# The gates' variance kept in a PSUM bank, and one Newton step written with the variance as a factor of its first operation

## What is computed

```python
x = x + conv(_ln_c(x), Wk, bk, Wq, bq, Wv, bv, Wr, br)      # linear attention, 8 heads, over the 16384 pixels
t = _to_tokens(x)                                           # (4, 16384, 64)
t = t + ffn(_ln_t(t), router_w, router_b, expert_w, expert_b)

def _ln_t(v, eps=1e-05):
    return (v - v.mean(-1)) / sqrt(v.var(-1) + eps)

def ffn(x, ...):                                            # B, N, D, C, E, K = 8, 4096, 64, 64, 8, 2
    router_probs = softmax(x @ router_w + router_b)
    top_p, top_i = top_k(router_probs, K); top_p /= sum(top_p)
    return sum over the two chosen experts of top_p * (x @ expert_w[e] + expert_b[e])
```

## Time and profile before

| | |
|---|---|
| median of 3 runs | 662.58 us (661.94 to 663.03) |
| profiled execution, its own time | 661.13 us |
| its span (first to last instruction) | 659.3 us |
| PE busy | 612.2 us (93%) |
| DVE busy | 506.5 us (77%) |
| ACT busy | 420.3 us (64%) |
| POOL busy | 396.4 us (60%) |
| granted TensorE clock, mean over the span | 0.991 |

### The profile page before, as it was taken

How to read it: one execution, slowest core, us unless ns; L and a number is a source line. 1 busy time by engine, 2 the same in 40 slices (tenths; PEclk the granted TensorE clock), 3 DMA queues, 4 the chain that set the end, 5 groups by cost and what they waited for, 6 DMA issues and landing times.

```text
span 659.3 us, 21452 instructions
## 1 busy us (share of the span) xinstructions
PE 612.2 (93%) x8318; PEld 277.4 (42%) x8318; DVE 506.5 (77%) x1176; ACT 420.3 (64%) x800; POOL 396.4 (60%) x350
## 2 busy tenths in 40 slices
PE   3799989779999999999999999999999999999997
PEld 1566656444444444444444444444333333332232
DVE  3434444798888888898888888988798999989954
ACT  2265646576767676766676676775857667676552
POOL 7223252127666566667666566656677767777986
PEclk9999989799999999999999999999999999999999
DMA  6132535395555566655556665544565667545652
GB/s 151 33 100 67 146 100 130 81 226 132 139 131 138 141 158 160 145 134 127 145 129 147 146 162 129 129 120 109 133 150 135 145 159 176 130 96 120 151 132 49
DMA packets 32663, 86.22 MB, mean 131 GB/s; under 512 B 7650, under 2 KB 7826, under 8 KB 32562
## 3 DMA queue, kind: packets, MB, share of 16 engines
q1 hardware_dynamic: 32082, 84.64, 53.4%
q0 software_dynamic: 288, 0.19, 0.2%
q10 hardware_dynamic: 192, 0.01, 0.0%
HBM read 34.47 MB, written 16.78 MB: 78 GB/s over the span
## 4 chain that ended last, share of the span: by engine, by line
PE 72%; DVE 18%; issue 6%; ACT 2%; POOL 2%; DVEq 0%; ACTq 0%; POOLq 0%
PE bank L1103 28%; PE bank L1089 8%; PE bank L1026 6%; PE bank L1004 5%; PE bank L990 5%; DVE z L834 4%; PE bank L949 3%; PE bank L973 3%; PE bank L1050 3%; PE bank L1100 3%; DVE x L734 2%; DVE osb L844 2%; PE bank L1075 2%; DVE xnT L689 2%; DVE bank L749 1%
## 5 line engine op out<-in xcount | busy, mean ns | idle before, releaser
L442 POOL TENSOR_TENSOR z<-gbs,x1d 128x512 f32<-128x512 f32 x256 | 320.6, 1278 | 170.8 <-ACT gbs L579 78.0
L1106 PE MATMUL bank<-z,ew 128*64 128x512 f32 x512 | 244.6, 599 | 0.0
L1103 PE MATMUL bank<-z,ew 128*64 128x512 f32 x512 | 243.6, 598 | 0.0
L579 ACT COPY gbs<-bank 128x512 f32<-128x512 f32 x256 | 140.9, 595 | 46.4 <-PE bank L1089 46.0
L834 DVE TENSOR_TENSOR z<-bank,x1d 128x512 f32<-128x512 f32 x256 | 165.3, 678 | 6.3 <-PE bank L1089 6.3
L433 POOL TENSOR_TENSOR xsq<-xin 128x512 f32<-128x512 f32 x64 | 65.4, 1044 | 85.0 <-DMA xin<-in_x_dram 67.4
L1103 PEld LDWEIGHTS bank<-z,ew 128*64 128x64 f32 x512 | 64.9, 136 | 103.4 <-issue 96.9
L1089 PE MATMUL bank<-grows,sel 64*64 64x512 f16 x1024 | 85.7, 387 | 6.1 <-ACT grows L573 4.8
L503 ACT COPY xn<-bank 128x512 f32<-128x512 f32 x64 | 34.4, 590 | 62.4 <-PE bank L949 62.4
L1106 PEld LDWEIGHTS bank<-z,ew 128*64 128x64 f32 x512 | 64.4, 136 | 1.1 <-POOL z L442 1.1
L734 DVE SCALAR_TENSOR_TENSOR x<-bank,br_col,x_again 128x512 f32<-128x512 f32 x64 | 45.0, 745 | 20.0 <-PE bank L1050 20.0
(11 more groups left out here) (135 smaller groups left out, 819.9 us busy)
## 6 DMA issues: line engine op xcount, KB each, us to landing
x1d<-x SPq DMA_DIRECT2D x128, 256.0 KB, 4.5
xin<-in_x_dram SPq DMA_DIRECT2D x64, 256.0 KB, 4.2
x_again<-in_x_dram SPq DMA_DIRECT2D x64, 256.0 KB, 4.1
out_dram<-osb SPq DMA_DIRECT2D x128, 128.0 KB, 2.6
k<-in_const_dram SPq DMA_DIRECT2D x1, 453.5 KB, 4.0
ew_nat<-in_L_ffn_expert_w_dram POOLq DMA_DIRECT2D x2, 64.0 KB, 6.4
sel<-in_const_sel_dram SPq DMA_DIRECT2D x1, 128.0 KB, 3.3
bk_rows<-bk_wide ACTq DMA_DIRECT2D x6, 1.0 KB, 1.7
```

Source lines behind the costliest of these rows:

```text
L442: pool.tensor_tensor(z[:, 1, i % R_Z, :], gbs[:, i % R_Z, :], x1d[:, g % 2, 1, u * NT:(u + 1) * NT], ALU.mult).then_inc(z_pool, 1)
L579: nc.scalar.copy(gbs[:, i % R_Z, :], bank[:, :]).then_inc(taken_of(("spread", i, 1)), 1)
L1103: pe.matmul(out_bank[0:C, :], ew[:, j, :], z[:, 0, i % R_Z, :], start=False, stop=(j == PAIRS - 1), skip_group_check=True).then_inc(prod_d ...
L1106: pe.matmul(out_bank[C:P, :], ew[:, j, :], z[:, 1, i % R_Z, :], start=False, stop=(j == PAIRS - 1), skip_group_check=True).then_inc(prod_d ...
```

## The change

The variance goes to a third strip of `dev_work` in bank 7 and no longer to `bstat[:, 1]` in SBUF. The three operations of Newton's step compute the same product in another order: before, -0.5 * r * r, times the variance, then plus 1.5 and times r; now -0.5 * variance * r, times r, then plus 1.5 and times r. The number of instructions, their order on every engine, their shapes and their semaphores stay as they are. Three of the 27 gate steps have operands in another memory:

| step | before | now |
|---|---|---|
| 2, clamp and epsilon | bank to SBUF | bank to bank |
| 3, reciprocal | SBUF to SBUF | bank to SBUF |
| 4, first of Newton | SBUF, SBUF to bank | bank, SBUF to bank |
| 5, second of Newton | bank, SBUF to bank | the same |

The other use of `newton`, for the statistics of x, is not touched, nor is step 0 (L749), whose two inputs are both in SBUF.

```diff
-        dev_work = [bank[7][:, QG * E + QG * i:QG * E + QG * (i + 1)] for i in range(2)]
+        dev_work = [bank[7][:, QG * E + QG * i:QG * E + QG * (i + 1)] for i in range(3)]
...
-                def rooted():
-                    dve.wait_ge(dev_root, p + 1)
-                    return dev[0]()
-
...
+                def gate_root():
+                    dve.wait_ge(dev_root, p + 1)
+                    return dve.scalar_tensor_tensor(dev_work[0], dev_work[2], -0.5, bstat[:, 3, :], ALU.mult, ALU.mult)
+
...
-                dev = newton(bstat[:, 0, :], bstat[:, 3, :], bstat[:, 1, :], dev_work)
                 steps = [
                     start,
                     lambda: dve.tensor_tensor(halves(dev_work[1]), halves(dev_work[0]), square, ALU.add),
-                    lambda: dve.tensor_scalar(bstat[:, 1, :], dev_work[1], 0.0, EPS_FFN, ALU.max, ALU.add),
-                    lambda: dve.reciprocal(bstat[:, 2, :], bstat[:, 1, :]),
-                    rooted, dev[1], dev[2],
+                    lambda: dve.tensor_scalar(dev_work[2], dev_work[1], 0.0, EPS_FFN, ALU.max, ALU.add),
+                    lambda: dve.reciprocal(bstat[:, 2, :], dev_work[2]),
+                    gate_root,
+                    lambda: dve.tensor_tensor(dev_work[1], dev_work[0], bstat[:, 3, :], ALU.mult),
+                    lambda: dve.scalar_tensor_tensor(bstat[:, 0, :], dev_work[1], 1.5, bstat[:, 3, :],
+                                                     ALU.add, ALU.mult),
```

## The result

| | before | changed | ratio (95% interval) |
|---|---|---|---|
| first comparison | 662.26 us (4 runs, 660.60 to 663.03) | 654.30 us (4 runs, 653.77 to 655.33) | 0.9885 (0.9862 to 0.9908) |
| second | 660.86 (17 runs) | 655.18 (6 runs) | 0.9908 (0.9883 to 0.9933) |
| third | 661.51 (11 runs) | 654.69 (6 runs) | 0.9894 (0.9865 to 0.9924) |
| fourth | 661.81 (17 runs) | 653.94 (5 runs) | 0.9885 (0.9848 to 0.9922) |

The fourth row is without one run of 662.26 us in the slow state. The kernel is faster, by 8.0, 5.7, 6.8 and 7.9 us.

What follows compares the result with a forecast made beforehand. PE was taken to set the pace, with VectorE mattering only where PE stops for it. Five quads at 1.22 us, 6.1 us in all, off the median 662.58 gave 656.5 us, range 655.3 to 660.3.

Steps and rivals of the forecast that it cites:

- The two holds: In five quads, gate step 4 and L657 on x's statistics wait for POOL's products; 0.97 and 1.03 us would go.
- the second rival: The hold doesn't depend on where inputs are, so new step 4 waits as before: 662.6 us, chance 0.03.
- `scale` gives part of it back: L767, two SBUF inputs, now comes inside POOL's second product and waits: 0.29 of step 4's 0.97 us given back.
- The second hold: L657 on x's statistics now passes before POOL's next pair in five quads, 1.03 us sooner; margin 0.57 us.
- the first rival: L657 on x's statistics still meets POOL's next pair, so nothing is gained: 662.6 us, chance 0.09.
- the form: The rival that the hold doesn't depend on where step 4's inputs lie: nothing gained, 662.6 us, chance 0.03.
- some of the five: Only some of the five held quads lose their stops; with half left 3.1 us gained, 659.5 us, chance 0.09.
- What PE makes of it: PE gains only its waits at L1036, L1089 and L966: 1.22 us in each of five quads, 6.1 us.
- The sum's base: The gain of 6.1 us was taken from the median of the runs, 662.58 us, giving 656.5.
- Steps 2 and 3: Gate clamp bank to bank, no change within 10 ns; reciprocal from the bank 4 ns longer; zero in the sum.
- The slower rival: The hold moves to untouched step 0 (L749) in the seven middle quads: +2.8 to +4.8 us, about 666, chance 0.05.

Runs made afterwards that it cites:

- order_only: The changed kernel with the variance back in SBUF and the new order of Newton's step kept: 661.46 us, ratio 1.0006 to the kernel before.
- four copies: The changed kernel with four unused bank-to-SBUF copies (128 x 160) on DVE ahead of the bias in five quads: 669.78 us, ratio 1.0109 to the kernel before.

## Why the prediction was right in its mechanism and missed its range

*The two holds.* Right. Step 4 no longer waits in any quad, and the row of the variance in SBUF brings the old time back. That the hold depends on two SBUF inputs rested on the association of rows before. It is shown now by step 4 in both forms (`order_only` differs from the changed kernel in the place of the variance alone), and step 0 in both forms agrees, though there the operation changed with its input. One reading of the prediction was wrong: the last Newton operation of the gates (L657, 191 to 192 ns) was not in POOL's company. POOL was busy during one of its 16 executions, and at 215.34 it stood idle between 215.02 and 216.67. So that row was next to no evidence, and the second rival deserved more than its 0.03; step 4 of the changed kernel is what tells, since POOL was busy beside eight of its 16 executions and none lasts over 200 ns. What stands ahead of the prediction, that the engines meet only at semaphores, is too narrow by this hold, which no semaphore shows (and not all engines write to SBUF here, as it has it: every PE row writes a bank). The page "SBUF — State Buffer" of the Trainium skill, in the section on SBUF's two separate sides, states it as a lock: a VectorE instruction with two SBUF inputs and a GpSimd instruction that reads SBUF exclude each other for a whole instruction, whichever starts first. The traces here agree for POOL in front (its products read `gbs` and `x1d` in SBUF); no run here singles out the other case. There is one addition: between two held operations in a row POOL gets in a whole product (1.18 and 1.19 us).

*`scale` gives part of it back.* Right: 0.70 us in the five quads, from 214.61 + 0.81 = 215.42 on.

*The second hold goes because DVE passes L657 ahead of POOL's pair, margin 0.57 us.* Right, and this was the step on which the gain hung. 0.48 us of added work left it alone and 0.72 brought it back with the whole time. So the first rival, that nothing is gained, comes true as soon as the margin is used up, and the 0.09 that it got was no formality. The rivals "the form" and "some of the five" didn't occur.

*What PE makes of it.* Here a term of the sum was mis-sized, 5 x 1.22 = 6.1 us where 6.65 was measured. I took 1.22 us a quad from the idle times in brackets. The start of L749 in two neighbouring quads gives what a quad takes. Before, with 212.22 from the earlier trace rows:

```profile
249.63 0.38 DVE L749 SCALAR_TENSOR_TENSOR bank<-lg 128x32 f32<-128x32 f32 x1
```

Changed:

```profile
213.03 0.38 DVE L749 SCALAR_TENSOR_TENSOR bank<-lg 128x32 f32<-128x32 f32 x1
```

```profile
249.12 0.39 DVE L749 SCALAR_TENSOR_TENSOR bank<-lg 128x32 f32<-128x32 f32 x1
```

37.41 against 36.09 us: 1.32 a quad, and 6.65 over the five, not 6.1. A PE wait is counted from the end of the last matmul, and an unheld matmul starts before that end: L1038 starts 0.64 us behind a group that lasts 0.71. The bracket of 0.83 us was a loss of 1.54 - 0.64 = 0.90. Over the whole stretch, from the transposition to the first expert product behind the three stops, before and changed:

```profile
222.40 0.59 PE L1103 MATMUL bank<-z,ew 128*64 128x512 f32 x1
```

```profile
221.65 0.59 PE L1105 MATMUL bank<-z,ew 128*64 128x512 f32 x1
```

222.40 - 217.89 = 4.51 against 221.65 - 218.70 = 2.95 us: the three stops of 1.22 us by their brackets cost 1.56. About 0.24 of it goes again some 6 us later, mostly where PE now starts the queries (L992, was L990) 0.36 and then 0.48 us behind the matmul before and not 0.24 and 0.43; what it waits for there was not followed up.

*The sum's base.* This is the larger part of the miss. I moved everything to the median of three runs, 662.58, which was a high one: with the fourth run it is 662.26, and in the three later comparisons the kernel before has 660.86, 661.51 and 661.81. From their mean of 661.4, less 6.65, comes 654.7, and the 21 runs of the changed kernel behind the four medians have one of 654.6. So of the 1.9 us between forecast and median about 1.2 are the base and about 0.5 the size of the term. The range had 0.5 us on the low side for the term, which was just enough, and 0.55 for the scatter, which was not.

On the profiled execution I forecast 655.0 us, and it took 655.33. That this fits is luck. With a gain of 6.65 it should have been 654.5, but the two profiles differ in the start as well. Between step 0 at 140 us and the next one, ahead of the seven quads, the kernel before took 35.2 us and the changed one 36.6. The granted clock between 140 and 150 us was full in the one and 0.83 in the other:

```profile
140.00:150.00 10.00, 8.53 (x177) 5.11 (x179) 8.05 (x23) 8.60 (x17) 3.85 (x4) 1.00 0.93 223
```

```profile
140.00:150.00 10.00, 8.52 (x145) 4.80 (x146) 7.63 (x20) 8.02 (x16) 3.43 (x3) 0.83 0.92 220
```

0.17 of 10 us would fit the 1.4 us, but the clock isn't the whole story. In the second comparison's profile of the changed kernel the clock was full there, and the stretch still took 36.5 us; PE stood for 1.27 us at L1006, for nothing that the profile shows:

```profile
150.79 0.97 PE L1006 MATMUL bank<-xnT,keys 128*64 128x66 f32 x25 [1.27 <-issue]
```

Of the twelve profiles of all kernels ten took 36.4 to 36.7 us for this stretch, and only those of the kernel before and of the changed one in the fourth comparison 35.2. So the profile on which the sum was built was a favourable one by 1.4 us. That is why the changed kernel's profile shows 5.8 us of gain with 6.65 in the five quads. What sets this stretch to one or the other stays open.

*Steps 2 and 3.* Right: the reciprocal from the bank takes 357 ns, and step 2 takes 199 ns where it took 191. The estimated 65 ns by the page "VectorE: DVE Perf Modes" of the Trainium skill, section on the TRN2 errata, don't show; the reciprocal is 4 ns longer.

*The slower rival.* L749 was held no longer than before (0.38 at 213.03), so DVE and POOL did move with PE. But slower was nearer than I thought, by another way: four copies, 0.97 us of DVE work where the margin is 0.57, give two holds in a row and 1.1% on the kernel before.

## What to carry to other kernels

In this kernel a small VectorE operation that comes while a GpSimd product runs costs whatever is left of the product, if both its inputs are in SBUF. A group whose longest time is near the duration of a GpSimd instruction is the sign. Putting one input in PSUM frees it, even at the price of one more small operation, but follow the chain to the next operation with two SBUF inputs: that one decides whether the gain is kept. For the gain on a pipelined PE take the distance between equal instructions of two periods, not the idle time in brackets. And before you build a forecast on one profile and three runs, ask how much the kernel scatters: here the base was off by twice as much as the term.

## What the runs showed of the hardware that was not expected

- Two dependent VectorE operations with two SBUF inputs, 0.17 us each when free, took 1.18 and 1.19 us: each waited for a product of its own of POOL's pair.
- Independent one-input VectorE operations of 0.32 us (128 x 160, bank to SBUF) started 0.24 us apart.
- Two of five stops of PE of 2.05 us were followed by a low granted clock (0.78, 0.50 and 0.87 in stretches of 2 us behind the one at 259.89 us), and three were not. The low clock cost 1.2 us each time. After the five stops of 0.83 us in the kernel before it stayed at 1.00.
